# Idle quarters of the input lend their memory to the last mixing: four spectra buffers and early-cleared staging tiles

## What is computed

```python
x_f = jnp.fft.rfft2(x)
k_f = jnp.fft.rfft2(weights)
out_f = jnp.einsum('bchw,ochw->bohw', x_f, k_f)
out = jnp.fft.irfft2(out_f, s=(H, W))
...
x = x + _L3_conv_ref(_gn(x), L3_conv_weights)
```

## Time and profile before

| | |
|---|---|
| median of three runs | 970.06 us (966.1 to 970.32) |
| profiled execution: time, span | 970.67 us, 968.9 us |
| TensorE busy | 782.8 us, 81% of the span |
| VectorE busy | 599.5 us, 62% |
| ScalarE busy | 517.0 us, 53% |
| mixing stage, first to last matmul | 776.7 to 870.0 us |
| TensorE idle in the mixing, by releaser | 10.1 us for the clearing on VectorE, 9.5 us for loads of spectra, 2.1 us "issue" |

### The profile page before, as it was taken

One profiled execution on the slowest core, in us unless ns is written; L12 is line 12 of the kernel. 1 busy time (PEld: TensorE's weight loads), 2 busy tenths in 40 slices (PEclk: granted clock), 3 DMA queues, 4 the chain that ended last, 5 costly groups with the idle time before them and its releaser, 6 DMA issues. The chain is left out here.

```text
span 968.9 us, 27289 instructions
## 1 busy us (share of the span) xinstructions
PE 782.8 (81%) x10775; PEld 654.1 (68%) x10775; DVE 599.5 (62%) x1112; ACT 517.0 (53%) x868; POOL 122.5 (13%) x120
## 2 busy tenths in 40 slices
PE   5999996853599665787599999984888588879998
PEld 5999995743588543666444444444777488879997
DVE  2555446655856689588777777776666677742222
ACT  0133246743443273465379999004887657765564
POOL 0000000100010044265301222100000100001110
PEclk9999998987789989699799999997999789999999
DMA  7499968532000010000000000004000448831222
GB/s 278 181 342 362 315 206 215 126 87 74 4 1 0 15 26 0 1 1 0 0 2 1 1 1 1 1 1 104 2 0 0 87 88 175 179 81 40 101 107 100
DMA packets 44553, 80.08 MB, mean 83 GB/s; under 512 B 19130, under 2 KB 37568, under 8 KB 40656
## 3 DMA queue, kind: packets, MB, share of 16 engines
q1 hardware_dynamic: 27856, 62.48, 22.7%
q10 hardware_dynamic: 16640, 16.78, 5.1%
HBM read 50.74 MB, written 27.92 MB: 81 GB/s over the span
## 5 line engine op out<-in xcount | busy, mean ns | idle before, releaser
L1462 DVE SCALAR_TENSOR_TENSOR X<-bank,c_power,X 32x512 f32 x128 | 96.8, 756 | 36.5 <-PE bank L1412 32.9
L914 DVE TENSOR_TENSOR X<-X,bank 128x512 f32 x64 | 43.6, 682 | 92.1 <-PE bank L900 92.1
L1605 PE MATMUL bank<-m_xp,m_kf 128*32 128x64 f32 x2048 | 81.7, 246 | 21.7 <-DVE m_xp L1540 10.1
L1605 PEld LDWEIGHTS bank<-m_xp,m_kf 128*32 128x32 f32 x2048 | 80.7, 172 | 22.9 <-issue 22.8
L429 ACT COPY ks_spec<-bank 128x512 f32<-128x512 f32 x64 | 34.3, 589 | 98.6 <-PE bank L357 98.6
L411 DVE COPY ks_rows<-bank 128x512 f32<-128x512 f32 x64 | 41.2, 687 | 70.9 <-PE bank L342 70.9
L215 DVE BATCH_NORM_STATS2 bn<-X 128x6 f32 x128 | 83.1, 683 | 2.9 <-POOL X L1202 1.6
L342 PE MATMUL bank<-ks_fw,ks_src 64*128 64x64 f32 x1024 | 68.7, 298 | 11.2 <-DMA ks_src<-in_L_conv_weights 11.2
L1368 ACT ACTIVATE c_r<-X,c_nrm 32x1024 f32 (+1 forms) x56 | 75.1, 1341 | 2.5 <-DVE c_nrm L1436 1.1
L342 PEld LDWEIGHTS bank<-ks_fw,ks_src 64*128 64x128 f32 x1024 | 68.1, 215 | 11.2 <-issue 11.2
L357 PE MATMUL bank<-ks_fh,ks_rows 64*128 64x128 f32 (+1 forms) x1152 | 71.2, 277 | 0.1
(11 more groups left out here) (186 smaller groups left out, 1869.2 us busy)
## 6 DMA issues: line engine op xcount, KB each, us to landing
ks_src<-in_L_conv_weights SPq DMA_DIRECT2D x8, 2048.0 KB, 8.2
kf<-ks_spec ACTq DMA_DIRECT2D x16, 1024.0 KB, 9.3
m_kf<-kf SPq DMA_DIRECT2D x32, 512.0 KB, 8.5
X<-in_x SPq DMA_DIRECT2D x4, 2048.0 KB, 13.8
out_y<-X SPq DMA_DIRECT2D x16, 512.0 KB, 2.6
xf<-f_xm SPq DMA_DIRECT2D x6, 448.0 KB
l_wb<-in_L_conv_weights_r SPq DMA_DIRECT2D x4, 512.0 KB, 11.0
l_wb<-in_L_conv_weights_i SPq DMA_DIRECT2D x4, 512.0 KB, 13.3
```

The lines of the kernel that those rows point to most:

```text
L914: dve.tensor_tensor(x, x, ps[4 + c % 4][:], ALU.add).then_inc(added, 1)
L1462: dve.scalar_tensor_tensor(x, of.rearrange("p (y x) -> p y x", x=HN), filt.power[at, 2:3], x, ALU.mult, ALU.add).then_inc(added, 1)
L1605: last = pe.matmul(ps[4 * half + m // 8][at:at + C, m % 8 * N:(m % 8 + 1) * N], kf[p][:, j, :, H * half + m], xp[half][:, j, m].rearrange( ...
```

## The change

It does five things.

1. In the forward stage, SP stores quarters 1, 2 and 3 of `X` to a new DRAM tensor `xs` as soon as each has been normalised, three DMAs of 2 MB.
2. Spectra buffers go from two to four: `kf0`, `X[:, 1]`, and two of their own. The loads of the first two pairs of units are both issued in the forward stage, the next two at the start of the mixing, and each of the other four when the pair of units four before it is done.
3. The staging tiles `xp` lie in `X[:, 3]` and `X[:, 2]`. POOL clears both in the forward stage, when the quarter's store has landed. The clearing at the start of the mixing is gone, on POOL and on VectorE.
4. TensorE's loop in the mixing has 2 iterations with the code of eight units each, since the buffer is part of an instruction's address. SP's loop is written out.
5. At the end of the mixing SP loads the three quarters back, after units 12, 15 and 16. In the inverse stage VectorE waits for its quarter (`present`), SP waits for all three before its first store.

```diff
-def l3_forward_stage(pr, mats, xm, kf0, loaded0):
+def l3_forward_stage(pr, mats, xm, ring, xp, loaded, zeroed):
...
-                load_kernel_spectra(sp, pr, kf0, 0, 0, loaded0)
+                load_kernel_spectra(sp, pr, ring[0], 0, 0, loaded[0])
+                for q in range(1, Q):
+                    for c in range(NCH):
+                        sp.wait_ge(fwd.ready[c], q + 1)
+                    sp.dma_start(pr.xs[q - 1], pr.X[:, q]).then_inc(spilled[q], 16)
+                    if q == 1:
+                        sp.wait_ge(spilled[1], 16)
+                        load_kernel_spectra(sp, pr, ring[1], 0, 1, loaded[1])
+
+            block.gpsimd
+            def _(pool):
+
+                for q, half in ((2, 1), (3, 0)):
+                    pool.wait_ge(spilled[q], 16)
+                    pool.memset(xp[half][0:2 * C, :, :, 1], 0.0).then_inc(zeroed, 1)
+                    pool.memset(xp[half][2 * C:P, :, :, 0], 0.0).then_inc(zeroed, 1)
...
-        kf = [kf0, pr.sb(ctx, "m3_kf1", [P, 2, C, N])]
-        xp = [pr.sb(ctx, f"m3_xp{p}", [P, 2, H, 2, 2 * B]) for p in range(2)]
+        kf = ring + [pr.sb(ctx, f"m3_kf{n}", [P, 2, C, N]) for n in (2, 3)]
...
-                load_kernel_spectra(sp, pr, kf[1], 0, 1, loaded[1])
-                with sp.Fori(1, PAIRS) as i:
-                    for p in range(2):
-                        sp.wait_ge(mixed, START + UNITS * i + 2 * p - 2)
-                        load_kernel_spectra(sp, pr, kf[p], i, p, loaded[p])
-
-            block.gpsimd
-            def _(pool):
-                clear(pool, 0).then_inc(zeroed, 1)
+                for n in range(2, 2 * PAIRS):
+                    if n >= 4:
+                        sp.wait_ge(mixed, START + 2 * (n - 4) + 2)
+                    load_kernel_spectra(sp, pr, kf[n % 4], n // 2, n % 2, loaded[n % 4])
+                for q, units in ((1, 12), (3, 15), (2, 16)):
+                    sp.wait_ge(mixed, START + units)
+                    sp.dma_start(pr.X[:, q], pr.xs[q - 1]).then_inc(restored[q], 16)
...
-                    if l == 1:
-                        clear(dve, 1).then_inc(zeroed, 1)
...
-                pe.wait_ge(zeroed, 2)
-                with pe.Fori(0, PAIRS) as i:
-                    for l in range(UNITS):
-                        p, half = l // 2, l % 2
+                pe.wait_ge(zeroed, 4)
+                with pe.Fori(0, PAIRS // 2) as ii:
+                    for l in range(2 * UNITS):
+                        n, p, half = l // 2, l // 2 % 2, l % 2
...
```

More of the change, by code:

```diff
@@ L191, in __init__ @@
         self.kf_stored = [self.sem(f"kf_stored{p}") for p in range(2)]
+        self.xs = nc.dram_tensor("xs", (Q - 1, P, PIX), F32, kind="Internal").ap()
         self.xf = nc.dram_tensor("xf", (Q, 2, C, KT, KX * 2 * IB), F32, kind="Internal").ap()
@@ L786, in _, with inverse_stage @@
                 pool.memset(y[:, :, KX:].rearrange("p s x r b -> p s (x r b)"), 0.0)
-def inverse_stage(pr, name, y, slots, modes, mats, rows4, last):
+def inverse_stage(pr, name, y, slots, modes, mats, rows4, last, restored=()):
     nc, ps = pr.nc, pr.psum
@@ L808, in inverse_stage @@
     pixels, added, step, stored = (pr.sem(f"{name}_{n}") for n in ("pixels", "added", "step", "stored"))
-    padded = pr.sem(f"{name}_padded")
+    padded, present = pr.sem(f"{name}_padded"), pr.sem(f"{name}_present")
     out_groups = pr.out.rearrange("(q b) c h w -> q (b c) (h w)", b=IB)
@@ L820, in _ @@
                 if last:
+                    sp.sem_inc(present, START)
+                    for r in restored[1:]:
+                        sp.wait_ge(r, 16)
+                        sp.sem_inc(present, 1)
                     with sp.Fori(0, Q) as q:
@@ L910, in _ @@
                 with dve.Fori(0, Q) as q:
+                    if last:
+                        dve.wait_ge(present, START + q)
                     for c in range(NCH):
@@ L1467, in _ @@
                     pr.group_stats(dve, q, step)
-def l3_forward_stage(pr, mats, xm, kf0, loaded0):
+def l3_forward_stage(pr, mats, xm, ring, xp, loaded, zeroed):
+    spilled = [None] + [pr.sem(f"f3_spilled{q}") for q in range(1, Q)]
     with ExitStack() as ctx:
@@ L1477, in _ @@
             def _(sp):
-                load_kernel_spectra(sp, pr, kf0, 0, 0, loaded0)
+                load_kernel_spectra(sp, pr, ring[0], 0, 0, loaded[0])
[6 more added lines that the diff above has]
+                        load_kernel_spectra(sp, pr, ring[1], 0, 1, loaded[1])
+            @block.gpsimd
+            def _(pool):
[3 more added lines that the diff above has]
+                    pool.memset(xp[half][2 * C:P, :, :, 0], 0.0).then_inc(zeroed, 1)
             @block.tensor
@@ L1503, in load_kernel_spectra, with l3_mix_stage @@
                              "(j c) t n -> c j (t n)", j=2)).then_inc(loaded, 16)
-def l3_mix_stage(pr, xm, kf0, loaded):
+def l3_mix_stage(pr, xm, ring, xp, loaded, zeroed, restored):
     nc, ps = pr.nc, pr.psum
@@ L1517, in l3_mix_stage @@
     H = N // 2
-    staged, copied, mixed, mixed_read, fix, zeroed = (pr.sem(f"m3_{n}") for n in (
-        "staged", "copied", "mixed", "mixed_read", "fix", "zeroed"))
+    staged, copied, mixed, mixed_read, fix = (pr.sem(f"m3_{n}") for n in (
+        "staged", "copied", "mixed", "mixed_read", "fix"))
     with ExitStack() as ctx:
-        kf = [kf0, pr.sb(ctx, "m3_kf1", [P, 2, C, N])]
-        xp = [pr.sb(ctx, f"m3_xp{p}", [P, 2, H, 2, 2 * B]) for p in range(2)]
+        kf = ring + [pr.sb(ctx, f"m3_kf{n}", [P, 2, C, N]) for n in (2, 3)]
         def spectrum(i, l, j, s2):
@@ L1535, in imaginary @@
             return xp[l % 2][(2 * s2 + 1) * C:(2 * s2 + 2) * C, j, :, s2]
-        def clear(eng, half):
-            eng.memset(xp[half][0:2 * C, :, :, 1], 0.0)
-            return eng.memset(xp[half][2 * C:P, :, :, 0], 0.0)
         with nc.Block() as block:
@@ L1544, in _ @@
             def _(sp):
-                load_kernel_spectra(sp, pr, kf[1], 0, 1, loaded[1])
-                with sp.Fori(1, PAIRS) as i:
-                    for p in range(2):
-                        sp.wait_ge(mixed, START + UNITS * i + 2 * p - 2)
-                        load_kernel_spectra(sp, pr, kf[p], i, p, loaded[p])
-            @block.gpsimd
-            def _(pool):
-                clear(pool, 0).then_inc(zeroed, 1)
+                for n in range(2, 2 * PAIRS):
[5 more added lines that the diff above has]
+                    sp.dma_start(pr.X[:, q], pr.xs[q - 1]).then_inc(restored[q], 16)
             @block.vector
@@ L1590, in _ @@
                 pr.keep_warm(pe, 16)
-                pe.wait_ge(zeroed, 2)
-                with pe.Fori(0, PAIRS) as i:
-                    for l in range(UNITS):
-                        p, half = l // 2, l % 2
+                pe.wait_ge(zeroed, 4)
+                with pe.Fori(0, PAIRS // 2) as ii:
+                    for l in range(2 * UNITS):
+                        n, p, half = l // 2, l // 2 % 2, l % 2
                         if half == 0:
[L1596 to L1600, removed]
+                            pe.wait_ge(loaded[n], 64 * ii + 64)
+                        pe.wait_ge(staged, 2 * UNITS * ii + l + 1)
+                        pe.wait_ge(copied, 2 * UNITS * ii + l + 1)
+                        pe.wait_ge(mixed_read, START + 2 * UNITS * ii + l - 1)
                         pe.sem_inc(pr.pace, 1)
@@ L1605, in _ @@
                                 last = pe.matmul(ps[4 * half + m // 8][at:at + C, m % 8 * N:(m % 8 + 1) * N],
-                                                 kf[p][:, j, :, H * half + m],
+                                                 kf[n][:, j, :, H * half + m],
                                                  xp[half][:, j, m].rearrange("p s n -> p (s n)"),
@@ L1687, in four_layers @@
             xm = pr.sb(layer, "xm", [P, SLOT // 4, N, 2, B])
+            restored = [None] + [pr.sem(f"m3_restored{q}") for q in range(1, Q)]
             inv, inv_loads = matrices(pr, layer, [("l3_ih", [P, P]), ("l3_ih0", [P, P]), ("l3_iw", [P, P])])
             with ExitStack() as inner:
-                kf0 = pr.sb(inner, "m3_kf0", [P, 2, C, N])
-                loaded = [pr.sem(f"m3_load{p}") for p in range(2)]
+                ring = [pr.sb(inner, "m3_kf0", [P, 2, C, N]),
+                        pr.X[:, 1].rearrange("p (j o k) -> p j o k", j=2, o=C)]
+                xp = [pr.X[:, q].rearrange("p (j k s n) -> p j k s n", j=2, s=2, n=2 * B) for q in (3, 2)]
+                loaded = [pr.sem(f"m3_load{p}") for p in range(4)]
+                zeroed = pr.sem("m3_zeroed")
                 fwd, fwd_loads = matrices(pr, inner, [(n, [P, 2, P]) for n in ("l3_fw16", "l3_fh16", "l3_fh016")], F16)
                 pr.stats_stage("n3", fwd_loads + inv_loads)
-                l3_forward_stage(pr, fwd, xm, kf0, loaded[0])
-                l3_mix_stage(pr, xm, kf0, loaded)
-            inverse_stage(pr, "i3", xm, SLOT, N, inv, 2, True)
+                l3_forward_stage(pr, fwd, xm, ring, xp, loaded, zeroed)
```

(2 more changed lines are left out.)

## The result

The changed kernel takes 978.75 us (median of 4 runs, 976.41 to 983.3), the kernel before 970.19 us in the same comparison. The ratio is 1.0081, with a 95% interval of 1.0048 to 1.0115: 0.5% to 1.2% slower. The profiled execution took 977.66 us with a span of 975.8 us.

What follows compares the result with a forecast made beforehand. TensorE was taken to bound the last mixing, a stage between two barriers, whenever it has data. Terms -7.7 - 9.5 - 2.1 + 10.1 + 2.1 + 11.5 sum to +4.4 us on 970.67: 975.1 us, range 950 to 986.

Steps and rivals of the forecast that it cites:

- Clearing gone: Start of the last mixing: without the clearing, TensorE's first matmul comes at 769.0 instead of 776.68, -7.7 us.
- Four buffers: Last mixing: two spare spectra buffers cover the transfers, so all five load waits of TensorE go, -9.5 us.
- Clock: TensorE in the mixing: removed load stops save 2.1 us of lowered clock; two new code stops cost 2.1 again.
- Code, first pass: First eight units of the mixing: eight code blocks late behind loads, 12.0 us less 1.93 already there, +10.1 us.
- The price of a block under load: First pass of the mixing: each code block fetched while loads are queued stops TensorE 1.5 us; rests on two packets.
- Code, second pass: Mixing loop's second pass: body not kept, code fetched again; 8.5 for the jump plus two stops of 1.5, +11.5 us.
- The two further stops: Rest of the mixing loop's second pass, after the jump: two more code stops of 1.5 us while DMAs run.
- Stores, clearing, reloading: Forward stage to inverse stage: storing, early clearing and reloading of X cost 0; bound +4 for the clearing.
- Rival B: Mixing loop: code stays, no second fetch, first pass as forecast; 963.6 us (957 to 971), chance 0.22.
- C: Mixing: code costs nothing, the late packet at 794 was a single bad case; 949.4 us, chance 0.13.
- D: Mixing: VectorE's staging becomes the bound under unbroken DMA traffic, 7 us more; 982 us and more, chance 0.05.

Runs made afterwards that it cites:

- e9_two: e11_ring_free with at most two 512 KB DMAs of spectra under way at a time: 958.31 us, ratio to before 0.9861.
- e3_quiet: Changed kernel without the six spectra loads in the mixing, so the output is not the layer's: 952.47 us, ratio 0.9814.
- e11_ring_free: Changed kernel with three of four buffers filled in the forward stage, 16 units written out, X reloaded after the last unit, loads issued whole: 965.36 us.
- e10_halves: e9_two with DMAs of 256 KB, two under way at a time: 949.38 us, ratio to before 0.9779.
- e1_body8: Kernel before with only TensorE's mixing loop changed, to two passes of eight units instead of four of four: 987.78 us, ratio 1.0179.
- e12_loop: e10_halves with TensorE's mixing code again a loop of two passes of eight units: 954.49 us, ratio to before 0.9822.
- e7_short7: e3_quiet with 56 of 64 matmuls in each unit, body of 7.1 blocks: one profile, no kernel time given, stop of 3.56 us at the branch.
- e8_short6: e3_quiet with 48 of 64 matmuls in each unit, body of 6.1 blocks: one profile, no kernel time given, no code packet from 800 to 838 us.
- e2_clear2: Changed kernel with two spectra buffers and TensorE's loop of four units, keeping early clearing and X's storing and reloading: 964.76 us, ratio to before 0.9933.

## Why the prediction held

- *Clearing gone*, -7.7: measured -8.1. VectorE's copies were undisturbed, as assumed.
- *Four buffers*, -9.5: all five waits went, -9.5.
- *Clock*, -2.1 and again +2.1: measured +3.2 in all. This term was mis-sized. Both stops of before that cost clock are gone, but stops of 3 us and more came in their place oftener than the two I counted. Nor does the length of a stop decide as I had read it, dips behind 2.05 us and none behind 1.96: the stretch behind the stop of 2.94 us was granted 1.00, that behind 3.00 us 0.76, and in e9_two the stretch behind a stop of 1.90 us 0.79.
- *Code, first pass*, +10.1 (12.0 of stops): measured 16.0 us of stops, +14.1. The cause is shown by e3_quiet (no loads, no stops) and by e11_ring_free, e9_two and e10_halves (stops by depth of queue). The price of a block under load, which I named as the weakest number, was 1.5 us for each of eight; it measured 2.0, in six stops of 2.7 on average. The 4.0 us in which a block comes in an empty queue is the longest of the five spacings in the first layer's trace; the others are 3.5 to 3.8.
- *Code, second pass*, +11.5: measured +8.8, all at the jump (expected 8.5). e1_body8 shows the loop's length as the cause, e12_loop the price of the jump with short queues, e7_short7 and e8_short6 the length at which a loop is lost. It was not a matter of a few waits over eight blocks: the body of 7.1 is fetched again too. The two further stops did not come, as no load followed the one that landed at 840.4.
- *Stores, clearing, reloading*: 0. e2_clear2, which has them all, is faster than before; a cost of a microsecond or two it would not show.

Rival B fell by the packets (57), C by the stops, D too: VectorE kept staging ahead of TensorE, which waited for it once, at the start. The sum was +4.4; the errors of the four terms (-0.4, +3.2, +4.0, -2.7) make +4.1, together the +8.5 of the mixing. The profiled executions differ by 977.66 - 970.67 = 7.0 us, since the part ahead of the mixing was 1.1 us shorter in the one after and the part behind it 0.4.

The mechanism of the loss was right, code that comes late behind loads and a loop that is fetched again. That the time came so near owes something to luck. The first pass and the clock cost 7.2 us more than I had put, and the second pass 2.7 less; without that the changed kernel would have lain some 3 us further off. I forecast 0.5% slower; it is 0.8%.

## What to carry to other kernels

Unrolling a loop to reach more buffers is a change of code length: count the records of the body and ask whether the code of a second pass is still there, and what the queues carry while it is fetched. TensorE's idle time named "issue", evenly spaced in records, with a packet of the instruction queue beside each, is code that arrives late. Deep queues of large DMAs make it late; where the transfers have slack, small pieces with two under way can give it back. Here that drew a load out from 10 to some 15 us, which the buffers covered but for 0.6 us, and the stops were gone.

## What I had not expected of the hardware

- A lone DMA of 512 KB takes 4.6 to 4.7 us from issue to landing where the earlier trace rows has 8.5 for four together, so issuing one by one halves the rate: 18.7 us for 2 MB instead of 10 to 11.
- A loop body 7.1 blocks long is fetched again as a whole (eight packets in its second pass, a ninth right behind), not only the part that was pushed out.
- How late a code packet is depends on the depth of one other queue: stops of up to 4.4 us with 2 MB in it, up to 1.9 with 1 MB at the same share of the DMA engines, none with 512 KB. Why the hardware serves the queues so, no run here shows.
